# Graph attention and a routed feed-forward layer: optional gathers behind the sixth, one-hots by ScalarE, byte targets

## What is computed

```
xp    = layernorm(x) @ W                              # 12500 x 4 x 64
alpha = leaky_relu(a_src[src] + a_dst[dst])           # per edge and head, with self loops
w     = softmax of alpha over the edges of a target
x     = x + elu(sum over edges (xp[src] * w) + bias)
n     = layernorm(x);  weights = n @ wr + br
sel   = the 6249 rows of n with the largest weights
x     = x + n + (gelu(sel @ w1 + b1) @ w2 + b2) * weight, the last term for the chosen rows alone
```

## Time and profile before

| | us |
|---|---|
| median of 3 runs | 2207.15 (2205.14 to 2212.3) |
| the profiled execution, span from first to last instruction | 2573.5 |
| its own time outside the profiler | not given; its span stands for it |
| TensorE busy (matmuls) | 1981.2 (77%) |
| VectorE busy | 1581.4 (61%) |
| GpSimd busy | 1554.5 (60%) |
| ScalarE busy | 744.5 (29%) |
| DMA, mean over the span | 143 GB/s |

### The profile page before, as it was taken

The page is one execution under the profiler, slowest core; times in us unless marked ns, Lnnn a source line. Parts: engine busy times, 40 slices in busy tenths (PEclk is TensorE's granted clock), DMA queues, the critical chain, the costliest instruction groups (busy, mean ns, idle before and its releaser), DMA issues.

```text
span 2573.5 us, 29095 instructions
## 1 busy us (share of the span) xinstructions
PE 1981.2 (77%) x9511; PEld 1633.8 (63%) x9512; DVE 1581.4 (61%) x3510; ACT 744.5 (29%) x1478; POOL 1554.5 (60%) x1626
## 2 busy tenths in 40 slices
PE   8935877877877877878778877877777777877787
PEld 6723666666666666666666666666666666666666
DVE  4555655665655655656656665666665665666576
ACT  4512222222322222322232232232232232223223
POOL 2366666666666666666666666666666666666630
PEclk9967988888888889889888888988988988889889
DMA  8844444444444444444444444444444444444447
GB/s 287 276 143 121 123 134 124 132 138 120 137 138 118 132 135 124 135 140 120 134 137 128 130 136 124 134 134 130 128 134 131 127 139 124 131 136 136 119 159 312
DMA packets 157137, 369.12 MB, mean 143 GB/s; under 512 B 46646, under 2 KB 73682, under 8 KB 155699
## 3 DMA queue, kind: packets, MB, share of 16 engines
q0 software_dynamic: 75088, 208.19, 30.1%
q1 hardware_dynamic: 74706, 145.62, 16.9%
q10 hardware_dynamic: 7184, 13.41, 1.4%
HBM read 328.20 MB, written 38.89 MB: 143 GB/s over the span
## 4 chain that ended last, share of the span: by engine, by line
POOL 38%; issue 23%; PE 19%; another core or an unknown queue 9%; DVE 3%; DMA 3%; ACT 2%; POOLq 1%; DVEq 0%; SPq 0%; ACTq 0%
POOL rows L692 38%; PE ag_ps L1057 7%; PE h_ps L1021 4%; PE ag_ps L934 3%; PE y_ps L1040 3%; DMA rows<-node_rows,ends 3%; POOLq L402 1%; DVE oh L1366 1%; DVE rows L1404 1%; ACT hT L808 1%; PE ag_ps L1128 0%; ACT L808 0%; PE ag_ps L1129 0%; ACT L812 0%
## 5 line engine op out<-in xcount | busy, mean ns | idle before, releaser
L692 POOL DMA_INDIRECT rows<-node_rows,ends x1563 | 1512.9, 968 | 850.6 <-issue 482.5
L1057 PE MATMUL ag_ps<-rows,oh 128*128 128x260 f32 x3518 | 845.9, 401 | 47.5 <-DVE rows L1404 34.8
L1021 PE MATMUL h_ps<-xnT,w1s 128*128 128x256 f32 x1568 | 534.0, 500 | 419.2 <-DVE zz L1385 227.1
L1057 PEld LDWEIGHTS ag_ps<-rows,oh 128*128 128x128 f32 x3518 | 716.7, 204 | 180.3 <-DVE rows L1404 37.8
L1021 PEld LDWEIGHTS h_ps<-xnT,w1s 128*128 128x128 f32 x1568 | 377.0, 250 | 517.9 <-DVE zz L1385 234.8
L1404 DVE TENSOR_TENSOR rows<-rows,xl_ps 128x512 f32<-128x512 f32 (+3 forms) x392 | 503.1, 1346 | 47.2 <-issue 26.5
L1385 DVE TENSOR_TENSOR zz<-rows,edge_dm 128x72 f32<-128x72 f32 x98 | 22.9, 233 | 695.0 <-DMA rows<-node_rows,ends 656.4
L1040 PE MATMUL y_ps<-w2s,hT 128*128 128x256 f32 x1568 | 368.0, 386 | 12.2 <-DVE oh L1366 9.2
L831 ACT COPY rows<-rows 128x780 f32<-128x780 f32 x97 | 81.6, 842 | 998.6 <-DMA rows<-node_rows,ends 998.6
L1040 PEld LDWEIGHTS y_ps<-w2s,hT 128*128 128x128 f32 x1568 | 301.7, 194 | 66.7 <-DVE oh L1366 16.6
L1366 DVE TENSOR_TENSOR oh<-xl_ps,dloc 128x2304 f32<-128x2304 f32 x98 | 249.0, 2541 | 0.0
(11 more groups left out here) (243 smaller groups left out, 1433.7 us busy)
## 6 DMA issues: line engine op xcount, KB each, us to landing
dbc<-dst SPq DMA_DIRECT2D x97, 576.0 KB
rows<-node_rows,ends POOLq DMA_INDIRECT x1563
selfr<-node_rows SPq DMA_DIRECT2D x98, 130.0 KB
base<-in_x SPq DMA_DIRECT2D x14, 896.0 KB, 7.1
base<-in_x SPq DMA_DIRECT2D x49, 256.0 KB
ffn_rows<-yb ACTq DMA_DIRECT2D x48, 256.0 KB
node_rows<-base SPq DMA_DIRECT2D x13, 910.0 KB, 5.7
base<-in_x_turned SPq DMA_DIRECT2D x14, 384.0 KB, 7.7
```

What stands on the lines that cost most here:

```text
L692: pool.indirect_dma_start(out=rows[:, b, t, :], out_offset=None, in_=table, in_offset=bass.IndirectOffsetOnAxis(ap=ends[:, b, t, 0:1], axi ...
L1021: last = nc.tensor.matmul(h_ps[:, m * PAIR:(m + 1) * PAIR], w1s[:, c, n * P:(n + 1) * P], xnT[:, c, :], start=(c == 0), stop=(c == DC - 1))
L1057: product = nc.tensor.matmul(ag_ps[b][:, 0:ROW], oh[:, b, t, :], rows[:, b, t, :], start=(t == 0), stop=False)
```

## The change

1. The optional gathers of a window (from the third window on) are issued right after its sixth regular gather (OPTIONAL = 5) instead of after the fifteenth. The wait for y_ok, which stood between the last regular and the first optional gather, stands at the head of the next window, ahead of its first gather, for the same value.
2. Waits of POOL with a fixed value are no longer instructions of their own (`held` instead of `wait_apart`): the gather behind them carries them.
3. The targets are stored and loaded as bytes, the lowest byte of each number (`dst8`, `low`), 288 KB broadcast per window instead of 576 KB, into the spare tile. SP's load waits for ScalarE's first pass over the same buffer (apart_ok) instead of lk_ok.
4. The one-hots `oht` are made by ScalarE, two passes per window: Square of the byte less the node's byte, then Relu of 1 - 2 times that. They are made for window w + 2, ahead of `exponentials(w + 1)`. VectorE keeps only the small subtractions of `one_hots_turned` (now `local_targets`).
5. `look_up` also waits for dm_ok of the window before; bank 0 of `hidden` waits for dm_ok instead of oht_ok.
6. The minimum with zero is taken of two tensors, the second being a column of zeros broadcast along the row.

```
-                sp.dma_start(dst16_dram.rearrange("(p e) -> p e", p=P), dst16).then_inc(d16_st, 16)
+                sp.dma_start(dst8_dram.rearrange("(p e) -> p e", p=P), dst8).then_inc(d16_st, 16)
...
-                    sp.wait_ge(lk_ok, w - 1)
+                    wait_apart(sp, (apart_ok, w - 1))
-                sp.dma_start(dbc[:, b, 0:flat], dst16_dram[...]...broadcast_to([P, flat])).then_inc(ld_dbc[b], 16)
+                sp.dma_start(low[:, b, 0:flat], dst8_dram[...]...broadcast_to([P, flat])).then_inc(ld_dbc[b], 16)
...
+            def held(w, semaphore, value):
+                if isinstance(w, int):
+                    pool.wait_ge(semaphore, value)
+                else:
+                    wait_apart(pool, (semaphore, value))
             def follow(w, started):
                 if started == LOOKED_UP:
-                    wait_apart(pool, (lk_ok, w + 1))
+                    held(w, lk_ok, w + 1)
                 for k in range(GROUPS):
                     if started == SUMMED[k]:
-                        wait_apart(pool, (freed[k], w))
-                if started == SECOND_LAYER and known(w, 5) and not (isinstance(w, int) and w == NW - 1):
-                    wait_apart(pool, (y_ok, w - 4))
+                        held(w, freed[k], w)
...
                 for t in range(3, tiles_of(w)):
-                    if known(w, 2) and t == 3:
-                        wait_apart(pool, (ld_ends[b], 16 * (i + 1)))
+                    if t == 3:
+                        if known(w, 6):
+                            held(w, y_ok, w - 5)
+                        held(w, ld_ends[b], 16 * (i + 1))
                     if known(w, 1):
                         follow(w, t - 3)
                     gather(t, gath[b])
+                    if known(w, 2) and t - 3 == OPTIONAL:
+                        optional(2)
...
+            def one_hots_turned(w, i, b):        # ScalarE
+                flat = tiles_of(w) * P
+                act.wait_ge(ld_dbc[b], 16 * (i + 1))
+                if known(w, 2):
+                    act.wait_ge(lk_ok, w - 1)
+                nc.scalar.activation(oht[:, b, 0:flat], low[:, b, 0:flat], ACT.Square, bias=minus_low[:, b:b + 1]).then_inc(apart_ok, 1)
+                act.wait_ge(apart_ok, w + 1)
+                nc.scalar.activation(oht[:, b, 0:flat], oht[:, b, 0:flat], ACT.Relu, bias=1.0, scale=-2.0).then_inc(oht_ok, 1)
...
+                if not isinstance(w, int) or w + 2 < NW:
+                    one_hots_turned(w + 2, i + 1, b)
                 exponentials(w + 1, i + b, 1 - b)
...
                 pe.wait_ge(oht_ok, w + 1)
+                if known(w, 1):
+                    pe.wait_ge(dm_ok, w)
...
-                        pe.wait_ge(oht_ok, w + 3)
+                        pe.wait_ge(dm_ok, w + 2)
                     hidden(w - 3, 1 - b, i - 2 + b, (0,))
...
-                dve.wait_ge(ld_dbc[b], 16 * (i + 1))
-                nc.vector.tensor_scalar(oht[:, b, 0:flat], dbc[:, b, 0:flat], node_id[:, bass.ds(w, 1)], None, ALU.is_equal).then_inc(oht_ok, 1)
...
-                nc.vector.tensor_scalar(zmin[:, :], zag[:, :], 0.0, None, ALU.min).then_inc(zmin_ok, 1)
+                nc.vector.tensor_tensor(zmin[:, :], zag[:, :], zero.broadcast_to([P, D]), ALU.min).then_inc(zmin_ok, 1)
```

More of the change, by code:

```diff
@@ L22 @@
 I16 = mybir.dt.int16
+U8 = mybir.dt.uint8
 ALU = mybir.AluOpType
@@ L172, in build @@
         xdiff = sb("xdiff", [P, H])
-        column = sb("column", [P, 17])
-        rs1, rstd, sq, half, xloc, broken, broken_all, widest, in_order, first_f, length, nge, cur, kth, sixteen, always, first_block = (column[:, k:k + 1] for k in range(17))
+        column = sb("column", [P, 18])
+        rs1, rstd, sq, half, xloc, broken, broken_all, widest, in_order, first_f, length, nge, cur, kth, sixteen, always, first_block, zero = (column[:, k:k + 1] for k in range(18))
         xmax = sb("xmax", [P, H])
@@ L403, in entry, with counted_before @@
                                       skip_runtime_bounds_check_because="the window table holds counts and places of the edges' tiles, which lie within their number")
+        def counted_before(eng, w, k):
+            return eng.value_load(win[0:1, bass.ds(COLS * w + k, 1)], min_val=0, max_val=NW * EP // P)
         def optional_landed(eng, w):
-            landed = eng.value_load(win[0:1, bass.ds(COLS * w + 7, 1)])
-            return nc.s_assert_within(landed, 16, 16 * (NW + 3), skip_runtime_bounds_check_because="a parity's first node block has one gather or more, each later one two at most")
+            return eng.value_load(win[0:1, bass.ds(COLS * w + 7, 1)], min_val=16, max_val=16 * (NW + 3))
         def all_extra(eng):
@@ L693, in gather, with optional @@
                                             in_offset=bass.IndirectOffsetOnAxis(ap=ends[:, b, t, 0:1], axis=0)).then_inc(arrived, 16)
+                def optional(known_w):
+                    if known_w >= 1:
+                        held(w, carry_ok, w)
+                    if known_w < 1:
+                        pool.wait_ge(win_ld, 16)
+                    some = entry(pool, w, 5, 2)
+                    if known_w < 1:
+                        gather(2, gath_last[b])
+                        with pool.If(some > 0):
+                            gather(1, gath_last[b])
+                        with pool.If(some > 1):
+                            gather(0, gath_last[b])
+                    elif known_w < 2:
+                        gather(2, gath_last[b])
+                        with pool.If(some > 1):
+                            gather(1, gath_last[b])
+                    else:
+                        with pool.If(some > 0):
+                            gather(2, gath_last[b])
+                        with pool.If(some > 1):
+                            gather(1, gath_last[b])
                 for t in range(3, tiles_of(w)):
[L696 to L697 removed]
+                    if t == 3:
+                        if known(w, 6):
+                            held(w, y_ok, w - 5)
+                        held(w, ld_ends[b], 16 * (i + 1))
                     if known(w, 1):
@@ L888, in _ @@
             nc.scalar.preload_act_table_set(EXP_AND_LN)
+            act.wait_ge(minus_ok, 1)
+            for w in range(2):
+                one_hots_turned(w, 0, w)
             exponentials(0, 0, 0)
```

68 lines of the change are left out of this document (27 added, 41 removed).

## The result

The changed kernel takes **2222.15 us** (median of 4 runs, 2220.64 to 2225.13) against 2208.14 (2205.14 to 2212.3) of the kernel before: ratio **1.0061** [1.0049, 1.0073]. It is slower by 0.6%. The forecast was 1.0% faster, and 2222 lies outside its range.

What follows compares the result with a forecast made beforehand. POOL's gather spacing was taken as the bound. All terms were 0 on the timed run except less stretching of gathers by VectorE, -23 us: 2207 - 23 = 2184 us (-1.0%), range 2100 to 2214.

Steps and rivals of the forecast that it cites:

- Bound (the 0.1% agreement of two times): POOL: profiled span 2573.5 less 368.4 us of real waits gives 2205.1, the timed run, so gather spacing bounds.
- Rival B: POOL's stalls are real in the timed run; reordering opens the loop and TensorE bounds: 2017 us, chance 0.13.
- Waits on the gathers, bytes, dm_ok: POOL's waits carried by gathers, halved broadcast load, hidden's earlier wait on TensorE: each 0 in the timed run.
- ScalarE's one-hots: ScalarE gains two passes, 2.2 us each, 4.4 us a window, within 6.5 us of waiting before the carry copy: 0.
- Rival C: ScalarE becomes the bound, its passes ahead of carry copy and exponentials; with table loads 2233 us, slower; chance 0.13.
- L1355 no longer stretching gathers: VectorE's L1355 removed, so gathers beside it are no longer stretched: 98 x about 0.17 = 17 us gained.
- The 0.9 us of cover: With punctual signals, the wait for y_ok is over 0.9 us before POOL arrives there.
- L1449's minimum: VectorE's L1449 becomes a minimum of two tensors and stretches gathers less: 6 us gained.
- My bound of 32 us: If a second input doubled VectorE's 0.325 us minimum: +32 us, inside its 656 us idle; path bounds 0 and 32.
- POOL's order: Optional gathers behind the sixth, y_ok at the next window's head: shortens stalls, which the timed run lacks, so 0.
- What VectorE no longer does to POOL: Gathers stretched by VectorE's L1355 and L1449 get shorter: -23 us, between 0 and 29.7.
- Rival E: The change does nothing here; stretching shifts to the remaining VectorE operations: 2205 us, chance 0.12.

Runs made afterwards that it cites:

- b_loads: Kernel before with only its two loads of the window table bounded, written the changed kernel's way: 2215.25 us, ratio 1.0022.
- b_act: Kernel before with the bounded loads, byte targets and one-hots by ScalarE, with the waits on dm_ok: 2211.46 us, ratio 0.9999.
- a_nomin: Changed kernel with the minimum of one input (tensor_scalar) again: 2211.13 us, ratio 1.0004.
- a_noorder: Changed kernel with POOL's queue of before (optional gathers last, y_ok ahead of them, waits apart): 2218.69 us, ratio 1.0038.
- b_min: Kernel before with the bounded loads and the minimum of two tensors: 2227.74 us, ratio 1.0079.
- a_d1: Changed kernel with the reciprocal ahead of the residual done twice, same values: 2205.42 us, ratio 0.9972.
- a_early: Changed kernel with VectorE's value load of the optional gathers' count put ahead of its wait for the regular gathers: 2203.47 us, ratio 0.9973.

## Why the prediction was wrong

- **Bound (the 0.1% agreement of two times): right.** Where before's real waits are absent (b_loads, the changed kernel), the span agrees with the timed runs and idle is 0.305 us a gather. Rival B, stalls that are real in the timed run, fell: with no stalls the window is as long. The forecast of the profiled span (2400 to 2550) was too cautious; it is 2219.5.
- **Waits on the gathers, bytes, dm_ok: 0.** They were run only as part of others; nothing in those asks for a price, but no run shows them by themselves.
- **ScalarE's one-hots: 2.2 us a pass, hidden: right.** 2195 and 2118 ns, one table load beside them in the whole run, and 433.4 / 97 = 4.5 us a window are left before the carry copy. Rival C is out, though the sign was its.
- **L1355 no longer stretching gathers, -17: right in the gathers** (-16.6 in b_act), but the time got 3.8 of it. The 0.9 us of cover that I had worked out for y_ok in one window was a mean at best. A gain of 0.17 us a window doesn't use it up, but single windows had none to spare (19 that wait, up to 1.0 us), and I set neither against the gain.
- **L1449's minimum, -6: wrong in sign.** I asked whether the longer operation fits into VectorE's idle time, where it does. It takes 0.426 us instead of 0.325 and pushes what follows it by 0.1 us against the gathers: from a_nomin to the changed kernel the gathers held by the residual's last step lose 10.6 us instead of 4.6, with 57 instead of 63 of them. In time it cost 7.2 us (b_act to a_noorder), 11.0 (a_nomin) and 12.5 (b_min), more than the traces show in two of the three. My bound of 32 us counted the operation's length, not what it does to POOL. I had also read the rows wrongly: the gather of 1226.17 (1.17 us) wasn't stretched by L1449, which starts 0.39 us into it, but by the addition of gbs, which this line of before shows under way at its start; 1226.10 + 0.43 + 0.82 = 1227.35 against 1226.17 + 1.17 = 1227.34.

```profile
1226.10 0.43 DVE L1447 TENSOR_TENSOR steps_of_rows<-steps_of_rows,gbs 128x256 f32<-128x256 f32 x1
```

- **POOL's order, 0: wrong.** Less idle, as it should be (13.8 us from b_act to a_nomin), but the value load behind the landing shifts VectorE's work by 0.7 us to a place where the residual stretches two gathers.
- **The step that failed** is thus "What VectorE no longer does to POOL. [...] Sum -23": I treated stretching as a property of each VectorE operation, to be subtracted with it. It is a property of the place: a gather loses what is left of the operation that is under way as it starts, less 0.13 us, and moving VectorE's work by 0.2, 0.6 and -0.7 us took the changed kernel's 26.6 us of extra at the residual to 5.4, 4.9 and 17.7. Rival E, that stretching shifts to the remaining operations, names the mechanism, with too small a chance and a bound (2205) that took for granted that the sum of it can't grow.
- **Parts don't add.** The four alone, measured from before, the loads once and the others each from b_loads: 5.2 + (-3.8) + 12.5 + 8.7 = +22.6 us, the change +14.0.
- **The Trainium skill, "SBUF — State Buffer", Who interferes with whom,** says of a VectorE instruction in a two-port mode that whoever comes second blocks until the first one's instruction ends, and that issue order decides who blocks. I compared an operation's whole length with the 0.14 us and set the rule aside, where what counts is the part left when the gather starts: L1355 of 1213.22 ends 0.27 us into the gather of 1213.90, and that gather ends 0.82 us later. The fixed distance of a stretched gather's end to that operation's end, and VectorE's own 0.25 instead of 0.17 us in a_d1, agree with the page. The page also says that a tensor_tensor takes only the read side of the shared pair and, as an inference, that making descriptors needs the write side. The traces speak against this for these gathers: 76 of the 77 that started under the minimum of two tensors, and 469 of the 475 under the addition of gbs, were held. A gather also reads its row numbers (`ends`) from SBUF, and no run here tells which of its accesses is the one that waits.

**Open:** through what a two-input operation holds a gather; the traces tell which operations do, no edit took each out at a fixed place. The bounded loads' 5.2 us are also unexplained: around the residual the trace of before has 4.3 us of extra and b_loads 9.2 at the same place, but before's profiled execution was drawn out, so this is a hint and no proof. And 9 of b_min's 12.5 us stand in no trace.

## What to carry to other kernels

Where one engine paces the kernel at a fixed spacing and another one's work is started by its results, the second falls at the same place of every beat, and a few tenths of a microsecond before it can be worth 1% in either direction (0.1 us cost 0.3 to 0.6% here, 0.2 us gained 0.8%). Find the place (start of the work less start of the pacing instruction) before and after a change, and look which operation is under way as each pacing instruction starts; an edit that costs nothing by idle time isn't free. If a part that should gain doesn't, try a small delay ahead of the suspected work: it is a one-line test, and here it was a gain as well. Put value loads ahead of waits, not behind them.

## What the runs showed of the hardware

- A gather is held by a VectorE operation that is under way as it starts, until that operation ends; it then takes 0.82 us more, of its 0.947 alone. In the 15 profiles 2258 of the 2337 gathers that started under an operation with two inputs in SBUF and over 0.15 us to run took more than 0.97 us. So did 207 of 208 under L1355, a tensor_scalar, and none of the 6842 that started with VectorE idle. Under operations that read PSUM it was 107 of 9625, all in the four kernels with L1355, where the summing of the look-up products (edge_dm) was under way just ahead of it.
- Who starts first decides, to some hundredths of a microsecond. In a_early, windows whose addition of gbs starts 0.33 us into a gather have 0.17 us of extra, at 0.37 it is 0.21, at 0.41 0.25, one for one with the place; at 0.42 and 0.43 it is -0.01 (9 windows). Up to 0.41, L1485 starts 0.035 us or more before the next gather and holds it; behind that it starts 0.03 us or less before. The window shown above is one of these: the gather of 1216.23 takes 0.95, and L1485, which started 0.02 us before it, takes 0.48 instead of 0.42.
- The 0.305 us between two gathers didn't move in any of the 15 profiles, whatever stood in between: a register load, a branch, or a wait that was already through.
- A value load of VectorE behind a wait costs 0.7 us before the next operation.
- One profiled execution of a kernel can be 17% longer than its runs (2573.5 against 2207 us), with waits that are in no other profile; a second profile of nearly the same code would have told it before the prediction did.
